# A graph layer and a slice-attention layer on one core: edge lists on ScalarE's queue, four low halves on GpSimd

## The reference, cut to what matters

```python
x, src, dst = _rec_inputs()        # x [6250, 256], 106250 edges sorted by dst, one self loop per node
n = _layernorm(x)
agg = segment_sum(n[src], dst, num_segments=6250)
h = relu(agg @ W_rel + b_rel + n @ W_root)              # 512 wide
gates = h @ W_ih.T + b_ih + b_hh                        # i, f, g, o; f is not used
c = sigmoid(i) * tanh(g)
x = x + (sigmoid(o) * tanh(c)) @ W_fc + b_fc
m = _layernorm(x)
sw = softmax((m @ W_x + b_x) heads @ W_slice + b_slice) / temperature)     # 8 heads, 64 slices
tokens = sw.T @ (m @ W_fx + b_fx), normalised; attention among the 64 tokens of a head
x = x + (sw @ attended tokens) @ W_out + b_out
```

## Time and profile before

| | us |
|---|---|
| median of 3 runs | 1281.21 |
| the profiled execution | 1282.48 |
| its span | 1280.7 |
| TensorE busy in it | 1119.0 |
| GpSimd busy in it | 801.8 |
| VectorE busy in it | 836.5 |
| ScalarE busy in it | 623.5 |

### The profile page before, as it was taken

One profiled execution on the slowest core, in us unless ns is written; L12 is line 12 of the kernel. 1 busy time (PEld: TensorE's weight loads), 2 busy tenths in 40 slices (PEclk: granted clock), 3 DMA queues, 4 the chain that ended last, 5 costly groups with the idle time before them and its releaser, 6 DMA issues. The chain is left out here.

```text
span 1280.7 us, 26663 instructions
## 1 busy us (share of the span) xinstructions
PE 1119.0 (87%) x9821; PEld 975.2 (76%) x9821; DVE 836.5 (65%) x2587; ACT 623.5 (49%) x1250; POOL 801.8 (63%) x850
## 2 busy tenths in 40 slices
PE   1036789999899999999999999999998999999998
PEld 0034687878688977888787878787787878897798
DVE  3977546676567666766677566756675667646565
ACT  1773245454446455445545455445544554545332
POOL 4227777777777777777777777777777777500000
PEclk9998999999999999999999999999999999999999
DMA  7574344434544444444444444444444444323399
GB/s 244 194 272 122 100 131 145 137 114 146 145 131 120 145 147 135 136 125 145 147 133 118 146 145 136 124 135 145 137 134 123 147 136 135 101 67 96 117 336 292
DMA packets 89720, 188.47 MB, mean 147 GB/s; under 512 B 19155, under 2 KB 51897, under 8 KB 89607
## 3 DMA queue, kind: packets, MB, share of 16 engines
q0 software_dynamic: 39888, 108.97, 29.7%
q1 hardware_dynamic: 39144, 58.76, 14.3%
q10 hardware_dynamic: 10575, 19.20, 4.2%
HBM read 154.86 MB, written 32.00 MB: 146 GB/s over the span
## 5 line engine op out<-in xcount | busy, mean ns | idle before, releaser
L632 POOL DMA_INDIRECT ring<-table,sidx x813 | 779.8, 959 | 290.0 <-issue 290.0
L403 PE MATMUL ps<-h_h,wih_h 128*128 128x250 f32 x1200 | 339.9, 283 | 0.0
L404 PE MATMUL ps<-h_l,wih_h 128*128 128x250 f32 x1200 | 337.4, 281 | 0.0
L405 PE MATMUL ps<-h_h,wih_l 128*128 128x250 f32 x1200 | 337.3, 281 | 0.0
L403 PEld LDWEIGHTS ps<-h_h,wih_h 128*128 128x128 f32 x1200 | 231.1, 193 | 1.7 <-issue 0.5
L404 PEld LDWEIGHTS ps<-h_l,wih_h 128*128 128x128 f32 x1200 | 231.2, 193 | 1.1
L405 PEld LDWEIGHTS ps<-h_h,wih_l 128*128 128x128 f32 x1200 | 231.0, 193 | 0.0
L989 PE MATMUL ps<-ring,oneh 128*32 128x512 f16 x2321 | 148.0, 386 | 72.1 <-DMA ring<-table,sidx 46.9
L768 ACT ACTIVATE gate<-ps,bgate 128x250 f32<-128x250 f32 x300 | 124.2, 467 | 140.9 <-PE ps L405 140.9
L1426 DVE TENSOR_SCALAR oneh<-iota,didx 128x64 f16<-128x64 f16 (+2 forms) x1199 | 184.0, 258 | 0.9 <-issue 0.9
L989 PEld LDWEIGHTS ps<-ring,oneh 128*32 128x32 f16 x2321 | 61.6, 97 | 142.4 <-DMA ring<-table,sidx 61.8
(11 more groups left out here) (212 smaller groups left out, 2475.8 us busy)
## 6 DMA issues: line engine op xcount, KB each, us to landing
ring<-table,sidx POOLq DMA_INDIRECT x813
swt_d<-swt ACTq DMA_DIRECT2D x25, 500.0 KB
gate<-swt_d SPq DMA_DIRECT2D x19, 500.0 KB, 5.9
x_room<-in_x SPq DMA_DIRECT2D x12, 512.0 KB, 21.0
xn<-table SPq DMA_DIRECT2D x25, 224.0 KB
xin<-in_x SPq DMA_DIRECT2D x25, 224.0 KB
res<-xin SPq DMA_DIRECT2D x25, 224.0 KB
table<-tile_room SPq DMA_DIRECT2D x8, 512.0 KB, 4.8
```

The lines of the kernel that those rows point to most:

```text
L403: eng.matmul(dst, wh, xh, start=first, stop=False)
L404: eng.matmul(dst, wh, xl, start=False, stop=False)
L405: return eng.matmul(dst, wl, xh, start=False, stop=last)
L632: pool.indirect_dma_start(ring[:, j, :], None, table, bass.IndirectOffsetOnAxis(ap=idx, axis=0)).then_inc(done, 16)
```

## The change

The lists are issued by ScalarE, as the first thing in its program, after a wait for the two VectorE memsets of the lists' padding only (a semaphore of their own, `list_pads`). Each list goes in three parts: 112 rows, 6 rows, and the last row of 522 words. SyncE issues the 13 pieces of x without a wait and with nothing between them. The low halves of pieces 8 to 11 are computed by GpSimd, in its program between the 18 raw gathers and the table's gathers; VectorE leaves them out.

```diff
+    POOL_LOWS = (8, 9, 10, 11)
...
-            def load_all(to, t, done):
-                sp.dma_start(to[0:LP - 1, :], t[0:(LP - 1) * wide].rearrange("(p b) -> p b", b=wide)).then_inc(done, 16)
-                sp.dma_start(to[LP - 1:LP, 0:LREST], t[(LP - 1) * wide:E].rearrange("(p b) -> p b", p=1)).then_inc(done, 16)
-
-            load_chunk(0)
-            sp.wait_ge(pads_set, 4)
-            load_all(src_i, a["src"], ld_src)
-            load_chunk(1)
-            load_all(dst_i, a["dst"], ld_dst)
-            for k in range(2, NCH + 1):
+            for k in range(NCH + 1):
                 load_chunk(k)
...
             for j in range(RAW):
                 gather_x(j)
+            for k in POOL_LOWS:
+                ln_low(pool, k)
             pool.wait_ge(plan_done, 1)
...
         @block.scalar
         def _(act):
+            def load_all(to, t, done):
+                for u, v in ((0, 112), (112, LP - 1)):
+                    act.dma_start(to[u:v, :], t[u * wide:v * wide].rearrange("(p b) -> p b", b=wide)).then_inc(done, 16)
+                act.dma_start(to[LP - 1:LP, 0:LREST], t[(LP - 1) * wide:E].rearrange("(p b) -> p b", p=1)).then_inc(done, 16)
+
+            act.wait_ge(list_pads, 2)
+            load_all(src_i, a["src"], ld_src)
+            load_all(dst_i, a["dst"], ld_dst)
             act.wait_ge(consts, NCONST)
...
-                dve.wait_ge(done, 32)
+                dve.wait_ge(done, 48)
...
-                if k:
+                if k and k - 1 not in POOL_LOWS:
                     ln_low(dve, k - 1)
```

More of the change, by code:

```diff
@@ L313, in build_program @@
         pads_set, plan_v, plan_pe, plan_done = (sem(n) for n in ("pads_set", "plan_v", "plan_pe", "plan_done"))
-        list_f, list_pe, list_s, list_d = (sem(n) for n in ("list_f", "list_pe", "list_s", "list_d"))
+        list_pads, list_f, list_pe, list_s, list_d = (sem(n) for n in ("list_pads", "list_f", "list_pe", "list_s", "list_d"))
         ln_var, ln_sd, ln_rstd, ln_x, ln_last, ln_hi = (
@@ L473, in _ @@
             with sp.If(general):
+                sp.wait_ge(pads_set, 2)
                 for to, t, pad in ((srcp, a["src"], pad_src), (dstp, a["dst"], pad_dst)):
@@ L1257, in _ @@
             low = LP // WIN * WIN
-            dve.memset(src_i[low:LP, LREST:wide], 0).then_inc(pads_set, 1)
-            dve.memset(dst_i[low:LP, LREST:wide], N).then_inc(pads_set, 1)
+            dve.memset(src_i[low:LP, LREST:wide], 0).then_inc(list_pads, 1)
+            dve.memset(dst_i[low:LP, LREST:wide], N).then_inc(list_pads, 1)
             dve.wait_ge(consts, NCONST)
```

## The result

| | before | after |
|---|---|---|
| median of the runs | 1281.11 us (1280.95 to 1282.22) | 1268.96 us (1267.88 to 1271.01) |
| the profiled execution | 1282.48 us | 1271.01 us |
| its span | 1280.7 us | 1269.2 us |

The change is faster, by 12.2 us where 17.2 was forecast, and 0.46 us outside the range.

The account below looks back on a forecast made before the run. The start of GpSimd's table gathers was taken to fix the end. Lists 16.9 us plus low halves 0.5 us gave 17.4 us earlier, 1263.8 against the median, stated as 1264.0 us; range 1261.5 to 1268.5 us.

Parts of the forecast that it names:

- What bounds the kernel: GpSimd's table gathers run back to back from 84.53 us; each microsecond earlier there is one off the end.
- as long as TensorE is ready: Condition on an earlier gather start paying off; TensorE was given 2 us a turn to make itself ready.
- The lists: Moving list DMAs to ScalarE lets VectorE start piece 2's statistics at about 12.5 instead of 29.44, 16.9 us earlier.
- from about 3: When the sources' transfer was taken to start, at half of 247 GB/s beside x; landed by 6.5 or 7.5 us.
- the alternative with a third of the rate: Lists getting a third of 247 GB/s: sources in at about 8.2, destinations 13.3, piece 2 near 14.0.
- VectorE's order behind it: VectorE's sequence after the sources land: floats, piece 1, copy back, floats of destinations, then piece 2 at about 12.5.
- the bound, 15.4: Smallest gain from the lists: piece 2 starts 15.4 us earlier if lists get a third of the rate.
- The low halves: Four low-half subtractions move from VectorE to GpSimd at 2.1 us each; the last is ready 0.5 us earlier.
- the first rival: GpSimd and VectorE hold each other up during low halves; last one 1.6 us later, 1265.9 us; chance 0.2.
- x's whole backlog: Rival: ScalarE's queue served only behind x, lists in at 28 to 31 us, time 1281 to 1284; chance 0.05.
- set the start by their pace: Rival: GpSimd's low halves so slow they set the gathers' start; at 10 us each, 1291 us; chance 0.02.
- TensorE lost no turn: Rival: a 47.7 us TensorE turn among the last two costs up to 8 us, 1268 to 1270; chance 0.08.

Follow-up runs that it names:

- split_bias_late: `split_sp` with VectorE's bias rows moved from behind piece 9 to behind the rest's low half; 1264.21 us.
- queue_only: `lists_only` with each list in its old parts of 118 rows and 1 on ScalarE's queue; 1290.89 us, ratio 1.0087 to the kernel before.
- x_waits: `lists_only` with SyncE waiting, between its first and second piece of x, for the padding fills that the lists wait for; 1267.53 us.
- lists_only: The change without its GpSimd part: lists on ScalarE's queue in parts, VectorE computes all low halves; 1266.61 us, ratio 0.9885 to the kernel before.
- lists_bias_late: `lists_only` with VectorE's bias rows moved from behind piece 9 to behind the rest's low half; 1265.89 us.
- split_sp: The kernel before with lists still on SyncE's queue between x's pieces, but in parts of 112, 6 and 1 rows; 1264.72 us, ratio 0.9872.

## Why the prediction was right and wrong

**What bounds the kernel: right, within a limit.** From before (84.53) to `split_bias_late` (66.62) time less first gather stays between 1195.0 and 1198.5 us, in `queue_only` too, where the start is 11 us later. The limit wasn't seen: with the start at 62.18 it is 1202.6, and the four kernels with the bias rows late, whose nineteenth gather waits 2.14 us or more, already lie at the upper end, 1197.6 to 1198.5. The change itself doesn't meet this wait. The step "as long as TensorE is ready" left out that TensorE is also what frees the slots.

**The lists: mechanism right, the landing mis-sized.** "The sources have a piece of x beside them: half the rate gives 425 KB / 124 GB/s = 3.4 us from about 3, so 6.5, or 7.5 with a microsecond for the landing." Measured 9.19, beyond even the 8.2 of the alternative with a third of the rate. The half was nearly right (0.62 MB against 0.75 from 5 us on). The step that failed is "from about 3": the queue moved next to nothing until almost two pieces of x had gone, at about 5. With 5 in its place the same sum gives 8.4, or 9.4 with the microsecond, which no run shows by itself. That the start is not all of it is shown by `x_waits`, where the queue starts sooner and the cast does not; with x held back it was 7.06 or less. VectorE's order behind it ran as written (from the floats of the sources to piece 2: 5.4 forecast, 4.99 measured). Effect: piece 2 15.26 us earlier, not 16.9; the bound, 15.4, was nearly this.

**The low halves: the wrong sign.** "0.5 us earlier" came out as 1.2 to 1.5 later. GpSimd's 2.1 us were right (2.12 to 2.17). What failed is the sentence "The rows show a disturbance, but not a whole operation's worth": they do, in the rows of the changed kernel, 2.13 against 0.56 and 1.50 against 0.42. The earlier trace rows were the wrong neighbours: there GpSimd gathers, and does not read two tiles of SBUF beside VectorE. This was the first rival, given 0.2, and its 1.6 later than before agrees. The Trainium skill, SBUF — State Buffer, section "Who interferes with whom", has the second of the two wait for the whole of the first when a VectorE instruction with two SBUF inputs meets a GpSimd instruction that reads SBUF; the runs agree.

**The sum.** First gather forecast at 84.53 - 17.4 = 67.1, measured 71.02, 3.9 later: 1.7 from the landing (14.18 against 12.5), 2.2 from the second half (56.8 against 55.1 - 0.5). Of those 2.2 the hold-up explains the 0.5 not gained and 1.2 to 1.5; the rest, 0.2 to 0.5, is not settled; `lists_only`, without low halves on GpSimd, has as much (55.6 against 55.1). Each deviation alone lies in the range (1265.7 or 1266.2), and both together, 1267.9, still do. What carries the median past 1268.5 is one microsecond more. The train of gathers can hold it, 1028.05 us against 1026.19 in the profiled executions, spread along the run; but trains differ by as much from one execution to the next without a cause found here. In the kernels whose gathers meet no wait for a slot they take 1024.1 (`queue_only`) to 1028.1 us (`x_waits`), and `lists_bias_late` has 1031.1 in its profiled execution (1271.2 us), while another of its runs took 1265.83. So that the time lies just outside the range is partly chance; the two missed terms are not.

**The other rivals.** The lists did not wait for x's whole backlog (0.05); in `queue_only` something near it happened, with parts of 118 rows. GpSimd's low halves did not set the start by their pace. TensorE lost no turn: 182.55 us behind its last wait, 182.4 before.

## What to carry to other kernels

Before a transfer is moved to another queue, look at the DMA share while it runs: at 0.13 it is the number of rows that wants mending, and 112 + 6 rows on the old queue did more (`split_sp`, 16.1 us) than the new queue and the split together (`lists_only`, 14.2 us, both from 1280.81). Before work goes to an idle GpSimd, look which VectorE rows with two inputs in SBUF lie beside it, the smallest too, and not only how long it takes itself: here 0.56 us became 2.13. And when an early start stops paying, look for the first wait behind it: here it was a slot in a ring.

## What the runs showed that was not expected

- The list DMA issued behind two lists of 118 rows was held: 16.78 us on ScalarE in `queue_only`, 7.03 on SyncE before. In parts of 112 and 6 rows it took 0.27 us (change).
- A list on a queue of its own is cast later (9.2 to 9.7 us) than behind a piece of x on x's own queue (7.02), issued at the same time: its queue moves next to nothing until almost two pieces of x have gone, and then has about half.
- The store of 106 rows needs 7.6 us from issue to the first gather, as 96 + 10 rows 4.1.
- Three additions of 128x4 elements, 0.56 us alone, take 2.13 beside one subtraction on GpSimd.
